# Mamba queues reordered; four-direction scans fed with delta by DMA, with three PSUM banks for u

## The reference, cut to what matters

```python
# ss2d, for each direction k of 4 (rows, columns, and both backwards), L = 4096 positions
x_dbl = einsum('bkdl,kcd->bkcl', xs, xproj_w)         # R = 6 + N = 8 + N = 8 rows
dts   = einsum('bkrl,kdr->bkdl', x_dbl[:, :, :R], dt_w)
delta = softplus(dts + dt_b)                           # [96, L]
dA    = exp(delta[..., None] * A)                      # 96 channels x 8 states
dBu   = delta[..., None] * Bs * xs[..., None]
h_l   = dA_l * h_(l-1) + dBu_l                         # the scan, sequential in l
y_k   = sum over states of h * C
# then: the sum over k, + Ds*x, layernorm over channels, * silu(z), out_w; Mamba: one direction, 16 states
```

## Time and profile before

| what | value |
|---|---|
| median of 3 runs | 8701.9 us (8682.01 to 8725.95) |
| the profiled execution | 8697.11 us, of which span 8695.3 us |
| mean granted clock of PE | 0.87 |
| busy: PE, DVE, ACT, POOL | 80%, 76%, 59%, 63% |
| first scans to last: Mamba, `scan_a`, `scan_b` | 69.8 to 3127.8, 3400.3 to 5205.2, 5363.2 to 7161.1 us |
| DMA over the span | 824 MB, 95 GB/s |

### The profile page before, as it was taken

One profiled execution on the slowest core, in us unless ns is written; L12 is line 12 of the kernel. 1 busy time (PEld: TensorE's weight loads), 2 busy tenths in 40 slices (PEclk: granted clock), 3 DMA queues, 4 the chain that ended last, 5 costly groups with the idle time before them and its releaser, 6 DMA issues. The chain is left out here.

```text
span 8695.3 us, 106513 instructions
## 1 busy us (share of the span) xinstructions
PE 6918.3 (80%) x18992; PEld 2411.2 (28%) x18992; DVE 6648.0 (76%) x7701; ACT 5164.0 (59%) x10686; POOL 5442.0 (63%) x4360
## 2 busy tenths in 40 slices
PE   7777887678778846888888877888888876889776
PEld 2222222122222212222222222222222222446332
DVE  6999999699999972888888993888888994532536
ACT  6777767577777743556666664556666664221556
POOL 5888888588888832677777872777777871000415
PEclk8888888788888867899999998999999998995788
DMA  4444344344434443333333432334333432374322
GB/s 92 102 94 108 94 103 106 72 100 97 109 95 102 107 111 86 76 79 92 87 83 83 94 83 58 80 80 95 90 86 86 98 88 63 129 234 121 96 59 74
DMA packets 439606, 824.00 MB, mean 95 GB/s; under 512 B 51879, under 2 KB 119836, under 8 KB 434268
## 3 DMA queue, kind: packets, MB, share of 16 engines
q1 hardware_dynamic: 439324, 821.20, 39.0%
HBM read 669.22 MB, written 151.79 MB: 94 GB/s over the span
## 5 line engine op out<-in xcount | busy, mean ns | idle before, releaser
L600 POOL TENSOR_TENSOR mamba_prod<-mamba_hs,mamba_BC_rep 128x512 f32<-128x512 f32 x1536 | 1933.2, 1272 | 389.4 <-DVE mamba_hs L552 359.0
L552 DVE TENSOR_TENSOR_SCAN mamba_hs<-mamba_dA,mamba_carry,mamba_dbx 128x512 f32<-128x512 f32 x1152 | 1463.8, 1271 | 0.0
L1550 POOL TENSOR_TENSOR scan_a_prod<-scan_a_hs,scan_a_BC_rep 128x512 f32<-128x512 f32 x768 | 980.8, 1277 | 475.1 <-DVE scan_a_hs L1476 378.3
L1550 POOL TENSOR_TENSOR scan_b_prod<-scan_b_hs,scan_b_BC_rep 128x512 f32<-128x512 f32 x768 | 980.6, 1277 | 467.9 <-DVE scan_b_hs L1476 375.3
L491 ACT ACTIVATE mamba_dA<-mamba_delta_rep,mamba_a_neg 128x512 f32<-128x512 f32 x1536 | 1090.2, 711 | 133.1 <-DVE mamba_hs L552 131.9
L539 DVE TENSOR_TENSOR mamba_dbx<-mamba_u_rep,mamba_BC_rep 128x512 f32<-128x512 f32 x1152 | 788.8, 685 | 326.2 <-PE mamba_u_rep L314 144.4
L282 PE MATMUL mamba_pre<-mamba_h,mamba_w_conv 96*96 96x512 f32 x1024 | 585.2, 712 | 329.2 <-POOL mamba_tails L568 279.2
L1857 POOL TENSOR_TENSOR ffn_sq<-ffn_xm 96x512 f32<-96x512 f32 x64 | 66.3, 1036 | 1156.0 <-DVE ffn_xm L1825 1146.5
L314 PE MATMUL mamba_u_rep<-mamba_du,mamba_sel 96*128 96x512 f32 x768 | 493.9, 730 | 160.8 <-DVE mamba_hs L552 153.6
L1322 ACT ACTIVATE scan_a_dA<-scan_a_delta_rep,scan_a_a_neg 128x512 f32<-128x512 f32 x768 | 519.0, 678 | 153.5 <-PE scan_a_delta_rep L1109 139.6
L1322 ACT ACTIVATE scan_b_dA<-scan_b_delta_rep,scan_b_a_neg 128x512 f32<-128x512 f32 x768 | 519.0, 678 | 148.3 <-PE scan_b_delta_rep L1109 134.4
(11 more groups left out here) (369 smaller groups left out, 14018.5 us busy)
## 6 DMA issues: line engine op xcount, KB each, us to landing
mamba_BC_rep<-bc_units SPq DMA_DIRECT2D x256, 512.0 KB, 10.3
scan_a_BC_rep<-bc_rows SPq DMA_DIRECT2D x512, 256.0 KB, 5.0
scan_b_BC_rep<-bc_rows SPq DMA_DIRECT2D x512, 256.0 KB, 4.9
mamba_delta_rep<-delta_units SPq DMA_DIRECT2D x512, 192.0 KB, 3.6
delta_units<-mamba_delta SPq DMA_DIRECT2D x128, 192.0 KB, 6.8
by_n<-fin_res SPq DMA_DIRECT2D x32, 768.0 KB, 3.3
fmid_src<-by_n SPq DMA_DIRECT2D x32, 768.0 KB, 6.2
by_k<-fmid_res SPq DMA_DIRECT2D x32, 768.0 KB, 4.3
```

The lines of the kernel that those rows point to most:

```text
L552: nc.vector.tensor_tensor_scan(hs[:, s % RING_H], dA[:, s % RING_A], dbx_bank(s)[:], carry[:, bass.ds(at, 1)], op0=ALU.mult, op1=ALU.add). ...
L600: pool.tensor_tensor(prod[:, (G * u + s) % RING_P], hs[:, s % RING_H], BC_rep[:, u, QUADS + s % QUADS], ALU.mult).then_inc(s_prod, 1)
L1550: pool.tensor_tensor(prod[:, (G * k + s) % RING_P], hs[:, (G * k + s) % RING_H], BC_rep[:, k, 2 + s % 2], ALU.mult).then_inc(s_prod, 1)
```

## The change

**`ss2d_phase`, delta.** PE no longer replicates delta. POOL writes delta into `dbc`, where ACT puts B and C below it; SP stores the 112 rows (`store_rows`) and reads them back with eight DMAs: four write delta over the partitions into an SBUF tile `delta_rep`, four write B and C as before (`spread`). ACT takes dA from SBUF. The tile ring of the states shrinks from 8 to 6, and several work tiles share memory.

**PSUM.** The two banks of `delta_rep` become a third bank of `u_rep` and a second of `dbx_even`. `rep_input` for the next step is issued right after the scan that frees its bank, a whole step ahead of its use. An even `times_b` waits for the scan four groups back instead of the one just ended.

**Layernorm and output.** The subtraction goes into PE's matrix (`centre_w` = identity - 1/96) and ACT copies and squares the bank (the square moves one group forward); `normalise` goes to POOL (group 17); `finish` goes to ACT (`evict_out`, group 23), and in `scan_b` PE adds the residual by an identity product. Only the last 8 outputs keep DVE.

**SP.** The convolution's input slab is loaded in the step k = 1 of the block before.

**`mamba_phase`.** `affine` goes from group 16 to 12, `tail` from 13 to 10.

```diff
@@ mamba_phase, ACT and POOL
-                elif s == 16:
+                elif s == 12:
                     affine(m)
...
-                elif s == 13:
+                elif s == 10:
                     tail(m)
@@ ss2d_phase, tiles
-    RING_H = 8
+    RING_H = 6
...
-        delta_rep = [p.ps(f"delta_rep{k}") for k in range(2)]
-        u_rep = [p.ps(f"u_rep{k}") for k in range(2)]
-        dbx_even = p.ps("dbx_even")
+        dbc = p.sb("dbc", [C + 2 * N, 2, T])
+        delta_rep = p.sb("delta_rep", [128, D, BLOCKS, T])
+        u_rep = [p.ps(f"u_rep{k}") for k in range(BLOCKS)]
+        dbx_even = [p.ps(f"dbx_even{k}") for k in range(2)]
@@ SP
-            def store_bc(k, count):
-                sp.wait_ge(s_bc, count)
-                sp.dma_start(bc_rows[k], bc[:, k % 2]).then_inc(s_bc_out, 16)
+            def store_rows(k, count):
+                sp.wait_ge(s_delta, count)
+                sp.dma_start(proj_rows[k], dbc[:, k % 2]).then_inc(s_out_rows, 16)
+
+            def spread(k, count):
+                sp.wait_ge(s_out_rows, count)
+                by_state = proj_rows[k, C:C + 2 * N].rearrange("(a n) t -> n a t", n=NB)
+                by_block = proj_rows[k, 0:C].rearrange("(b c) t -> c b t", c=32)
+                for n in range(NB):
+                    sp.dma_start(delta_rep[32 * n:32 * n + 32, k], by_block).then_inc(s_rep_d, 16)
                 for n in range(NB):
                     sp.dma_start(BC_rep[32 * n:32 * n + 32, k], by_state[n].unsqueeze(0).broadcast_to([32, 4, T])
                                  ).then_inc(s_bc_rep, 16)
...
+                    if k == 1 and has_conv:
+                        sp.wait_ge(s_conv, done_slab)
+                        load_slab(at_slab)
@@ PE
-                nc.tensor.matmul(pre[1][0:C], mean_w[:], Y[:, bass.ds(at, T)], start=True, stop=True
+                nc.tensor.matmul(pre[1][0:C], centre_w[:], Y[:, bass.ds(at, T)], start=True, stop=True
...
-                        if s % 2 == 0 and (s + 4 < G or has_next or k + 1 < D):
-                            if s + 4 == G:
-                                pe.wait_ge(s_delta, j + 2)
-                            pe.wait_ge(s_dA, q + 2)
-                            rep_delta(k if s + 4 < G else (k + 1) % D, (s // 2 + 2) % BLOCKS)
-                        if s % 2 == 1 and (s + 3 < G or has_next or k + 1 < D):
-                            if s + 3 == G:
+                        if s % 2 == 1 and (has_next or k + 1 < D):
+                            if s == 1:
                                 pe.wait_ge(s_du, j + 2)
                             pe.wait_ge(s_scan, q + 1)
-                            rep_input(k if s + 3 < G else (k + 1) % D, (s + 3) // 2 % BLOCKS)
+                            rep_input((k + 1) % D, s // 2)
@@ ACT
+            def evict_out(f):
+                act.wait_ge(s_out, f + 1)
+                wait(act, s_store, 16 * f)
+                if residual is None:
+                    nc.scalar.activation(xo[:, :, 1:HW + 1], split(pre[1][0:C]), ACT.Copy).then_inc(s_xo, 1)
+                else:
+                    nc.scalar.activation(xres[:], pre[1][0:C], ACT.Copy).then_inc(s_xo, 1)
...
-                        act.wait_ge(s_rep_d, BLOCKS * j + s // 2 + 1)
+                        if s == 0:
+                            act.wait_ge(s_rep_d, 64 * (j + 1))
...
-                        if has_out and at == 16:
+                        if has_out and at == 15:
                             square(f)
+                        if has_out and at == 23:
+                            evict_out(f)
@@ DVE
                 if g % 2 == 0:
-                    wait(dve, s_scan, G * j + g - 1)
+                    wait(dve, s_scan, G * j + g - 3)
...
-                        if has_out and k == 2 and s == 2:
-                            centre(f, *values(dve, f // CH % 2, f % CH))
-                        if has_out and k == 3 and s == 0:
-                            normalise(f)
-                        if has_out and k == 3 and s == 5:
-                            finish(f)
@@ POOL
             def add_softplus(j, slot):
                 pool.wait_ge(s_sp, j + 1)
-                wait(pool, s_rep_u, BLOCKS * (j - D + 1))
-                pool.tensor_tensor(du[:, slot, 0], sp_relu[:], sp_ln[:], ALU.add).then_inc(s_delta, 1)
+                pool.wait_ge(s_bc, j + 1)
+                wait(pool, s_out_rows, 16 * (j - 1))
+                pool.tensor_tensor(dbc[0:C, slot % 2], sp_relu[:], sp_ln[:], ALU.add).then_inc(s_delta, 1)
...
+                        if has_out and k == 2 and s == 5:
+                            normalise(f)
```

More of the change, by code:

```diff
@@ L906, in ss2d_phase @@
         xms, xhs, sqs, lnvs, rstds, yns, ygs = (
-            BC_rep[0:C, 0], BC_rep[0:C, 1], hs[0:C, 4:6], du[:, 0], hs[0:C, 0:3], dA[0:C], prod[0:C])
-        residuals = (xres, zraw, sp_abs, sp_exp)
-        mean_banks, var_banks, out_banks = (pre[0], delta_rep[0]), (u_rep[0], u_rep[1]), (dbx_even, pre[1])
+            BC_rep[0:C, 0], BC_rep[0:C, 1], hs[0:C, 4:6], du[:, 0:2], hs[0:C, 0:3], dA[0:C], prod[0:C])
+        residuals = (xres, zraw, sp_ln, sp_relu)
+        mean_banks, var_banks, out_banks = (pre[0], dbx_even[1]), (u_rep[0], u_rep[1]), (dbx_even[0], pre[1])
         s_frames = p.sem("frames")
@@ L918, in staggered @@
                         step(t - lag)
[L919 removed]
+        NW = 13
+        s_diag = p.sem("diag")
         PRE = 3
@@ L978, in load_out, with store @@
                                  ).then_inc(s_xres, 16)
-            def store(at, at_res):
+            def store(at, at_res, out):
                 if residual is None:
@@ L1046, in load_residual @@
                 if e < 4:
-                    wait(sp, s_xo if v == 0 else s_sz, TAIL)
+                    wait(sp, s_store if v == 0 else s_sz, 16 * TAIL if v == 0 else TAIL)
                 else:
@@ L1192, in _ @@
             pe.wait_ge(s_du, 1)
-            for c in range(2):
-                rep_delta(0, c)
+            for c in range(BLOCKS):
                 rep_input(0, c)
@@ L1203, in _ @@
                     pe.wait_ge(s_sz, TAIL + e - 1)
-                nc.tensor.matmul(split((y, delta_rep[1])[e % 2][0:C]), w_in[:, C:2 * C],
+                nc.tensor.matmul(split((y, u_rep[2])[e % 2][0:C]), w_in[:, C:2 * C],
                                  frames[:, e * ROWS:(e + 1) * ROWS, 1:HW + 1], start=True, stop=True
@@ L1368, in _ @@
                 act.wait_ge(s_z, TAIL + e + 1)
-                nc.scalar.activation(szs[:, e], (y, delta_rep[1])[e % 2][0:C], ACT.Silu).then_inc(s_sz, 1)
+                nc.scalar.activation(szs[:, e], (y, u_rep[2])[e % 2][0:C], ACT.Silu).then_inc(s_sz, 1)
             nc.scalar.preload_act_table_set(EXP_LN)
@@ L1476, in body @@
                         nc.vector.tensor_tensor_scan(hs[:, (G * k + s) % RING_H][:, way], dA[:, (2 * k + s) % 4][:, way],
-                                                     (dbx_even, u_rep[(BLOCKS * k + s // 2) % 2])[s % 2][:, way], carry[:, bass.ds(at + G * k + s, 1)],
+                                                     (dbx_even[(BLOCKS * k + s // 2) % 2], u_rep[s // 2])[s % 2][:, way], carry[:, bass.ds(at + G * k + s, 1)],
                                                      op0=ALU.mult, op1=ALU.add).then_inc(s_scan, 1)
```

141 lines of the change are left out of this document (67 added, 74 removed).

## The result

The changed kernel takes 8220.3 us (median of 4 runs, 8212 to 8223), the kernel before 8692.2 measured beside it (median of 4): ratio 0.9455, 95% interval 0.9441 to 0.9468. The prediction was 8210 with a range of 8060 to 8470; the time is 10 us above it. The profiled execution has a span of 8219.9 us, against 8695.3 before. About one run in ten, of the kernel before and of the experiments' kernels but none of the changed kernel's four, was 1.2 to 1.3% shorter than the others, in the two that were profiled all of it behind the second scan phase, which moves a median by some 5 us at most.

What follows compares the result with a forecast made beforehand. DVE's serial scans bound the scan phases, with waits for PE and ACT. From 8697.1 us, less 444 for two scan phases, plus 4 for their starts, less 50 for Mamba: 8207, predicted as 8210, range 8060 to 8470.

Steps and rivals of the forecast that it cites:

- The floor: Scan phases, DVE: 24 groups at 1.79 us plus 3.5 us for sums into `Y`, 46.5 us a block.
- PE's term: Scan phases: PE loses 14.1 us a block, `u_rep` is issued earlier, so DVE's 89 us of waits go.
- The rival of a slower clock: Scan phases: PE rests more, runs at 1.2 GHz, its results reach ACT some 1 us later; 8383 us, chance 18%.
- ACT's stalls: Scan phases: DVE's waits caused by ACT, 1.6 us a block convolving only, 4.1 doing both, 2.1 putting out only.
- Group 12: Scan phases: DVE's 2.5 us wait behind ACT's table loads shrinks to 1.5, or 0.9 without z.
- the 1.5 us for group 15 and for `affine`: Middle scan blocks: 1.0 for ACT's copy and square before the softplus, 0.5 for `affine` awaiting POOL's product.
- Group 23: Scan phases: new wait, `evict_out` waits for `project_out` and POOL's gate; 6.5 us against 5.4 of lead, 1.1.
- DMA: Scan phases: 2.23 MB a step takes 10.1 us plus 1.6 idle, 11.7 against 12.65 of compute; hidden.
- The estimate of 7.8 us: Scan-phase DMA at the skill page's 358 GB/s: 6.2 + 1.6 us a step, so DMA could never set the pace.
- The earlier slab: Scan phases: loading the convolution's slab half a block ahead was given no gain of its own.
- The slower-than-before rival: Scan phases: the store lands late behind the last step's loads, 15.9 us a step; 9105 us, chance 4%.
- Mamba: Mamba phase: earlier `tail` and `affine` cut DVE's `u_rep` waits; 25 us a layer, 50 for both, bounds 150 and -20.

Runs made afterwards that it cites:

- early-convolution kernel: Changed kernel with the convolution's ninth product issued at group 8, not 10, in the scan phases: 8164.5 us.
- the extra rows: Changed kernel with two further loads, 0.51 MB more DMA in each scan-phase step, into a tile nobody reads: 8548.3 us.
- the six profiles: Profiles of the changed kernel and five experiment kernels that keep its Mamba code: Mamba 3032 to 3056 us from first to last scan.
- the last kernel: Changed kernel plus Mamba B rows first, residual after step 1, output copy behind next dA tile 1, z copy tile 4, convolution groups 4 to 8: 8061.8 us.

## Why the prediction was right, step by step

**The floor** (DVE's own work in a block, without waits) was 46.5 us a block. From the windows less the waits it is 48.5 - 2.3 = 46.2, 49.9 - 3.6 = 46.3 and 46.6 - 0.6 = 46.0. Right; the pitch is 1.77 and not 1.79. The undone even wait costs 97 us net, some 137 in pace, where 123 were worked out. What the subtraction, the product and the output copy were worth to DVE (about 2 us a block by the prediction) no run shows by itself; only the floor as a whole was met.

**PE's term** named both the freed 14.1 us and the longer lead, and let the lead remove the 89 us. The experiment with three groups of lead shows that this was the right one. But PE's busy share was to be 72% and is 83%: its matmuls a block fell as expected (1603 in 760 us are 105 a block, 1571 in 700 were 129), and the `u_rep` products take 733 ns. The rival of a slower clock came true in part: 0.89 granted in the middle stretch against 0.93. By itself that makes 36.3 x 0.93/0.89 = 38 of the measured 631.62/15.2 = 41.6 us a block; what makes the rest is open. ACT's idle time for PE there (54.5, 50.0, 18.2, 7.6 and 6.0 us in 15.2 blocks) is 9.0 us a block, just under the 10 that the prediction named as that rival's sign, and it costs nothing at most places. The clock alone was no price: in the last stretch it was lowest, 0.80, and there DVE waits least, 0.6 us a block. Three of ACT's waits in the middle window:

```profile
ACT L1249 <- PE scan_a_pre L1085: 54.5, 16, 3.8
...
ACT scan_a_xm L1308 <- POOL scan_a_xm L1531: 31.0, 15, 2.4
ACT scan_a_xo L1296 <- PE scan_a_pre L1117: 18.2, 15, 2.4
```

The first row is group 12, the second `affine`, the third the output copy at group 23. The Trainium skill's "TensorE: Matmul & The Clock Gate", section "HAM oscillation — how this bites in real kernels", made PE's rests the danger. The trace agrees in kind: PE rested 89 of 700 us before, at 0.93, 128 of 760 after, at 0.89, and 74 of 340 in the last stretch, at 0.80. The price it does not bear out: the rival's was 8383 - 8207 = 176 us, and the dearest case on record, the second phase of the early-convolution kernel at 0.83, is 53 us longer than the first, with the clock as cause not shown.

**ACT's stalls** were 1.6, 4.1 and 2.1 a block and are 2.3, 3.6 and 0.6. The sum for the middle blocks is near by luck: one of its four pieces doubled, one came to two thirds and two never came. Group 12 was to shrink from 2.5 to 1.5, because one `delta_rep` pair leaves the convolution's way; it is 2.94. The failed step is "two to three tenths come back as DVE arrives sooner": 2.1 us came back. The last thing that PE waits for ahead of the convolution's end is scan 7, and from there it works without a rest. So the paths of ACT and of DVE can be counted from the end of scan 7. Before (scan 7; DVE's wait at group 11), and after (scan 7; the `u_rep` pair that it frees):

```profile
4289.05 1.27 DVE L1476 TENSOR_TENSOR_SCAN scan_a_hs<-scan_a_dA,scan_a_carry,scan_a_u_rep 128x512 f32<-128x512 f32 x1
4297.45 0.70 DVE L1420 TENSOR_TENSOR scan_a_dbx_even<-scan_a_u_rep,scan_a_BC_rep 128x512 f32<-128x512 f32 x1 [1.60 <-PE scan_a_u_rep L1113]
```

```profile
3990.77 1.29 DVE L1477 TENSOR_TENSOR_SCAN scan_a_hs<-scan_a_dA,scan_a_carry,scan_a_u_rep 128x512 f32<-128x512 f32 x1
3992.11 1.13 PE L1120 MATMUL scan_a_u_rep<-scan_a_du,scan_a_sel 96*128 96x512 f32 x2 [1.03 <-DVE scan_a_hs L1477]
```

To ACT's table load it was 4300.21 - 4290.32 = 9.89 us and is 4000.20 - 3992.06 = 8.14: 1.75 less, since two `delta_rep` pairs left the way and not one. To the point where DVE is ready for scan 13 it was 4305.01 - 2.52 - 4290.32 = 12.17 and is 4005.04 - 2.94 - 3992.06 = 10.04: 2.13 less, 1.60 of it the wait for `u_rep` at group 11, which the prediction itself had taken away in PE's term. The wait grows by the difference, 0.4, and it is the same in all 15 blocks of the stretch. Ending the convolution at group 8 took 2.04 us off the first path and cut the wait to 0.50. Against that, the 1.5 us for group 15 and for `affine` never came: ACT does wait for POOL's normalise, 2 us a block by the second of ACT's rows above, and catches up within its lead. Group 23, 1.1, is 0.7 (10 us in 15 blocks). In the last blocks the forecast 2.1 is 0.6.

**DMA.** 10.1 + 1.6 = 11.7 us a step, hidden: the experiment gives an estimate of 11.1. The share is 0.77 for 0.75. The estimate of 7.8 us, from the Trainium skill's "DMA: Bandwidth & Descriptors", section "Where 436 GB/s comes from", would have had the extra rows hidden (1.4 us more by its 358 GB/s, in a step of 12.5); they cost 328 us. Going by the rows was right.

**The earlier slab** was said to be "in the 58.2", nothing of its own. It is the prediction's largest omission and by luck cost it nothing, since the change has both parts: the rows by DMA fill the queue at a block's start, and the slab's move is what keeps PE from waiting behind it. The slower-than-before rival looked for the queue's harm in the store's landing; it would have been found here.

**Mamba** was 50 and is 15 in the first pair of profiles, 9 in the means, and not told from nothing. The third that "I give the convolution" was near: the waits for `u_rep` fell by 41 us (by 19 to 46 in the six profiles). The step that failed is counting them in full as time, for 26 came back as waits for `BC_rep`. I had asked what is late next in the scan phases and not in Mamba. The affine pass, whose move had the lower bound of -20, made neither gain nor loss in time.

So the 15 us between the sum of 8207 and the profiled 8222 are a balance: 26 us more gained in the scan phases, 35 less in Mamba, 6 lost in the rest. The mechanism of the scan phases held (pace, `u_rep`, hidden DMA); that the total came within 15 us is luck, as the errors at group 12, group 15, `affine` and in Mamba offset each other.

## What to carry to other kernels

When a change fills a DMA queue, follow every small load that is issued behind the big ones, and on the engine that waits for it count everything that stands behind the waiting instruction: here 253 KB in the wrong place were worth 381 of 472 us. Where the releaser of a wait has itself last waited for the bound engine, count both paths from that point: every pause that the change takes from the bound engine in between makes the wait longer (2.52 to 2.94 us here). Moving the work earlier in the releaser's order shortens it. And where a wait on one engine is taken away, ask which transfer was due just behind it.

## What the runs showed of the hardware

- One queue of 2 KB rows carries 210 to 220 GB/s with all 16 engines busy, 218 to 248 with the further loads; a load of 253 KB issued behind a spread of 1.84 MB was there 6.6 us later.
- The early-convolution kernel ran the middle of its second scan phase at a granted clock of 0.83, with `u_rep` pairs of 2.07 us after rests of 1.3 to 2.8 us among others of 1.1, and that of its first at 0.91. The phases differ by the residual: a load on SP, and one more product in front of the output. Moving the load left 0.85; new positions for two of ACT's copies and for the convolution brought 0.89. Whether the waits and the low clock keep each other alive, and why the first phase escaped, is open.
- A table load takes 1.28 us; two of them and two SiLUs, 3.8 us, fit into ACT's lead over DVE when the convolution's result is ready: in the last kernel DVE does not wait for ACT there.
- Exp on 128x512 from an SBUF tile took 712 ns (the changed kernel), from PSUM 678 ns (the kernel before).
